# Negated maximum as bias of four exps, and value products of attention in groups, in a post-norm decoder layer

## The chip, the cores and the metric

The kernel runs on one core of a Trainium2 chip. The metric is the device time of one launch in microseconds. Before the change it is 2332.79 us, the median of three runs (2332.78 to 2335.61).

The engines of a core are called here as the profile calls them: PE (matrix products, with its weight loads as PEld), DVE (vector engine), ACT (scalar engine), POOL (GpSimd), SP (the queue that issues DMAs). Each works through its own list of instructions in order; semaphores tie the lists together.

## The reference

One decoder layer on 32 batch items of 256 tokens with 256 features; all activations are float32.

```python
x = _layernorm(x + self_attention(x))            # 16 heads of 16, causal, with biases
x = _layernorm(x + cross_attention(x, ctx))      # 16 heads of 64, 77 context tokens
x = _layernorm(x + ffn(x))                       # weights of +1/-1: 512->1024->1024->256, relu twice

# cross attention, per head
scores = jnp.einsum('bhqd,bhkd->bhqk', q, k) * scale      # scale = 64 ** -0.5
attn = jax.nn.softmax(scores, axis=-1)                    # over 77 keys
out = jnp.einsum('bhqk,bhkd->bhqd', attn, v)
```

## The kernel before, in words

A first part (about 140 us) loads and splits the weights and computes keys and values of the context for all 32 items. Then `attention(i, f, g)` runs once per item `i`, 32 times. One pass of it holds, interleaved by hand, the self attention and the cross attention of item `i`, the scores of the self attention of item `i + 1`, two layers of the feed-forward part of item `f = i - 1` and the last layer of item `g = i - 2`. Each engine has its own function `attention`, and the order of the calls in it is that engine's order of work. Nothing else sets the order: there is no scheduler. The feed-forward products (`layer0`, `layer1`, `layer2`, called through `filler0`, `filler2` and `layer1_until`) stand where PE would otherwise wait.

The cross attention of an item works on eight blocks `t` of two heads with 256 queries, so that one block has 4 rows of 77 scores in each of 128 partitions. For a block these functions follow each other, one engine handing to the next:

- PE `cross_queries(u)` (L988, two blocks at a time), ACT `cross_queries(u)` copies them out of PSUM (L499).
- PE `cross_scores(t)` (L1130) writes PSUM bank 4 or 5 in turn, so block `t` can start when block `t - 2` has left its bank.
- DVE `cross_max(t)` (L736) and `cross_below(t)` (L742): the maximum, and scores minus maximum into `p2`. The second frees the bank (semaphore `d_b2`).
- ACT `cross_exp(t)` (L504) on `p2` in place, DVE `cross_sum(t)` (L748) and `cross_inverse(t)` (L753), POOL the product with the inverse (L419).
- PE `cross_transposes(t)` (L1141), ACT `cross_probs(t)` copies them out (L511), PE `cross_values(t)` (L1155), ACT `cross_output(u)` (L516) and DVE `cross_output_low(u)` (L758) for two blocks, PE `cross_projection(t)` (L1169).

`cross_values` has 77 rows by 64 columns of weights: head 0 of a block lands in the left half of PE's columns, head 1 in the right half. `values(g)` of the self attention (L1082) has 32 columns of weights, four heads side by side. The other products use all 128 columns, the transposes of L1141 77 of them.

In the self attention, PE `scores_by_key(n)` (L1069), ACT `self_probs(n)` (L524) and POOL (L412) make the probabilities of two heads in one of four buffers `pr`, and `values(g)` uses two of them.

Of the kernel before, what the change touches and what calls it, by code (L numbers as in the profile page):

```python
# [14 lines left out]
P = 128  # L15
# [10 lines left out]
def decoder_layer(nc, x, ctx, w_qkv, b_qkv, w_proj, b_proj, w_q, w_k, w_v, w_o, k0, k1, k2, s0, s1, s2, out):  # L26
# [22 lines left out]
    with ExitStack() as stack:  # L49
# [31 lines left out]
        max2 = sb("max2", [P, KX, 4], F32)  # L81
# [14 lines left out]
        with ExitStack() as first:  # L96
# [20 lines left out]
        probs = sb("probs", [P, 6, 512], F32)  # L117
        probs_flat = probs[:].rearrange("p a b -> p (a b)")
        pr = probs_flat[:, 0:4 * 768].rearrange("p (n a b) -> p n a b", n=4, a=2)
# [10 lines left out]
        p2 = sb("p2", [P, KX, 4, SK], F32)  # L130
        p2_t = sb("p2_t", [SK, 4, 512], F32)
# [49 lines left out]
        d_m2, d_b2, d_s2, d_i2, d_o2l, d_y2, d_x2, d_r0, d_r1, d_y3, d_out = (  # L181
            sem("d_" + n) for n in "m2 b2 s2 i2 o2l y2 x2 r0 r1 y3 out".split())
# [49 lines left out]
        SPLIT_SCALE = (1.0, 1.0, 1.0, CROSS_SCALE, 1.0)  # L232
# [149 lines left out]
        def _(pool):  # L382
# [24 lines left out]
            def attention(i, f, g, more=True):  # L407
                for n in range(NP):
                    pool.wait_ge(a_p, nth(i, NP, n + 1))
                    pool.sem_inc(passed_pool, 1)  # L410
                    diag = pr[:, n % 4, :, 0:2 * P].rearrange("p a (b q) -> p a b q", b=2)
                    pool.affine_select(out=diag, in_=diag, compare_op=ALU.is_ge, fill=0.0, base=0,  # L412
                                       pattern=[[0, 2], [0, 2], [1, P]], channel_multiplier=-1).then_inc(g_p, 1)
# [29 lines left out]
        def _(act):  # L443
# [74 lines left out]
            def self_probs(i, n):  # L518

                act.wait_ge(pe_st, nth(i, NP, n + 1))  # L520
                if n >= 4:
                    act.wait_ge(pe_pv, nth(i, 4, n // 2 - 1))
                b = 4 + 2 * (n % 2)
                act.activation(pr[:, n % 4, :, :], ps[:, b:b + 2, P:512], ACT.Exp, scale=SELF_SCALE).then_inc(a_p, 1)  # L524

            def self_output(i, m):

                act.wait_ge(pe_pv, nth(i, 4, 2 * m + 2))
# [7 lines left out]
            def attention(i, first, f, first_f=False, more=True):  # L536
# [98 lines left out]
        def _(dve):  # L635
# [126 lines left out]
            def attention(i, first, f, g, more=True):  # L762
# [9 lines left out]
                self_output(i, 0)  # L772
                if more:
                    transposed_x(i + 1)
                if not first:
# [28 lines left out]

                cross_max(i, 0)
                cross_below(i, 0)
                cross_max(i, 1)
                cross_below(i, 1)
                cross_sum(i, 0)
                if more:  # L810
                    self_max(i + 1, 0)
                for t in range(2, KX):
                    cross_max(i, t)
                    cross_inverse(i, t - 2)
                    cross_below(i, t)
# [118 lines left out]
        def _(pe):  # L934
# [138 lines left out]
            def values(i, g):  # L1073

                pe.wait_ge(g_p, nth(i, NP, 2 * g + 2))
                if g == 0:
                    pe.wait_ge(a_nm, nth(i, 2, 2))
                c = (g % 2) * S
                for b in range(TB):
                    for j in range(4):  # L1080
                        src = pr[:, (2 * g + j // 2) % 4, j % 2, (1 - b) * P:(3 - 2 * b) * P]
                        last = pe.matmul(ps[32 * j:32 * j + 32, 2 + g // 2, c + b * P:c + S], v[:, b, 4 * g + j, :], src,  # L1082
                                         start=b == 0, stop=b == 1)
# [39 lines left out]
            def cross_scores(i, t):  # L1123
# [3 lines left out]
                if t >= 2:  # L1127
                    pe.wait_ge(d_b2, nth(i, KX, t - 1))
# [16 lines left out]
            def cross_values(i, t):  # L1145

                u = t // 2
                pe.wait_ge(a_p2t, nth(i, KX, t + 1))
                if t % 2 == 0 and u < 2:
                    pe.wait_ge(a_q2, nth(i, 4, u + 3))  # L1150
                elif t % 2 == 0:
                    pe.wait_ge(a_o2h, nth(i, 4, u - 1))
                    pe.wait_ge(d_o2l, nth(i, 4, u - 1))
                for e in range(2):
                    last = pe.matmul(ps[64 * e:64 * e + 64, 6 + u % 2, (t % 2) * S:(t % 2 + 1) * S],  # L1155
                                     v2[:, (2 * t + e) * XD:(2 * t + e + 1) * XD], p2_t[:, t % 4, e * S:(e + 1) * S],
                                     start=True, stop=True)
                last.then_inc(pe_o2, 1)

            def cross_projection(i, t):  # L1160

                if t == 0:
                    pe.wait_ge(d_b2, nth(i, KX, KX))
# [19 lines left out]
            def attention(i, f, g, more=True):  # L1183
# [18 lines left out]
                values(i, 0)  # L1202
                filler2(2)
                scores_by_key(i, 4)
                if f is not None:
                    if g is not None:
                        pe.wait_ge(d_y3, nth(g, 2, 1))
                    transposed_x2(f)
# [176 lines left out]
```

## Time and profile before

| | |
|---|---|
| median of three runs | 2332.79 us |
| the profiled execution | 2333.06 us |
| its span, first to last instruction | 2331.3 us |
| mean granted clock of PE in it | 0.987 |
| PE busy | 2233.6 us, 96% of the span |
| DVE busy | 1485.0 us, 64% |
| ACT busy | 970.2 us, 42% |
| POOL busy | 482.0 us, 21% |

"Busy" counts the time in which at least one instruction of the engine is under way. PE's matmuls overlap in the records, since the next one starts while the results of the last still run out of the array; what an instruction costs PE is therefore read from the distance between two starts, not from its duration. On ACT and DVE also the next instruction starts before the last has ended, by about 0.1 us.

In the rows below `ps` is PSUM, `p` is the cross attention's `p2`, `p_t` its transpose, `q` the tile `q2`; `x8` means eight instructions merged into one row. A bracket at a row's end is idle time before it, and who ended it.

### The profile page before, as it was taken

How to read it: one execution, taken by the hardware profiler on the slowest of the kernel's cores; microseconds unless marked ns; L12 is line 12 of the kernel's file. 1: busy time of each engine (PE TensorE's matmuls, PEld its weight loads, DVE VectorE, ACT ScalarE, POOL GpSimd, SP SyncE). 2: the span in 40 equal slices, each digit the busy share in tenths (PEclk: the TensorE clock that was granted, in tenths of full speed). 3: DMA queues.
4: the chain of work that ended last, by engine and by line, in shares of the span. 5: the costliest groups of instructions: out<-in, count | busy, mean ns of one | idle time of the engine just before them, and what ended most of it. 6: DMA issues, size and time to landing. Idle time of an engine off the chain costs nothing.

```text
span 2331.3 us, 52778 instructions
## 1 busy us (share of the span) xinstructions
PE 2233.6 (96%) x18516; PEld 1847.7 (79%) x18516; DVE 1485.0 (64%) x4685; ACT 970.2 (42%) x1797; POOL 482.0 (21%) x751
## 2 busy tenths in 40 slices
PE   7967899999999999999999999999999999999997
PEld 6856787888888888788888888888888888888876
DVE  3435666667667666667676666676676666676763
ACT  3313444444444444444444444444444444444432
POOL 2001212222222122212222222222221222122220
PEclk9978999999999999999999999999999999999999
DMA  6753332132333331233333322323333212233300
GB/s 209 228 115 53 54 58 45 39 50 37 56 56 56 56 50 41 42 44 49 56 56 56 56 42 39 47 41 56 56 56 56 48 40 44 40 53 56 56 25 10
DMA packets 150504, 135.85 MB, mean 58 GB/s; under 512 B 47746, under 2 KB 141986, under 8 KB 150402
## 3 DMA queue, kind: packets, MB, share of 16 engines
q1 hardware_dynamic: 150468, 135.37, 31.3%
q8 instruction: 23, 0.38, 0.1%
q14 instruction: 13, 0.11, 0.0%
HBM read 39.10 MB, written 28.59 MB: 29 GB/s over the span
## 4 chain that ended last, share of the span: by engine, by line
PE 81%; DVE 10%; issue 4%; ACT 3%; DMA 2%; POOL 1%; SPq 0%; DVEq 0%; POOLq 0%
PE ps L1028 10%; PE ps L1029 9%; PE ps L1169 9%; PE ps L988 8%; PE ps L1155 6%; PE ps L1011 5%; PE ps L1141 4%; PE ps L1082 4%; PE ps L1069 4%; PE ps L997 4%; DVE max L736 3%; PE ps L1039 3%; PE ps L1040 2%; PE ps L970 2%; PE ps L977 2%
## 5 line engine op out<-in xcount | busy, mean ns | idle before, releaser
L1028 PE MATMUL ps<-r_h,w 128*128 128x256 f16 x2048 | 464.4, 274 | 1.9 <-DVE r_l L682 1.9
L1029 PE MATMUL ps<-r_l,w 128*128 128x256 f16 x2048 | 462.1, 273 | 0.0
L471 ACT ACTIVATE r_h<-ps 128x512 f16<-128x512 f32 x256 | 152.6, 596 | 524.1 <-PE ps L1029 516.4
L697 DVE CUSTOM_DVE_ANT_0 junk<-ps,causal 128x128 bf16<-128x128 f32 (+1 forms) x1024 | 316.2, 353 | 60.1 <-PE ps L1058 53.8
L419 POOL TENSOR_TENSOR p<-p,inv 128x308 f32<-128x308 f32 x256 | 179.0, 699 | 479.5 <-DVE inv L753 479.5
L682 DVE SCALAR_TENSOR_TENSOR r_l<-ps,r_h 128x512 f16<-128x512 f32 x256 | 176.1, 688 | 119.5 <-ACT r_h L471 119.5
L524 ACT ACTIVATE probs<-ps 128x768 f32<-128x768 f32 x256 | 206.9, 809 | 106.9 <-PE ps L1069 106.8
L412 POOL TENSOR_SCALAR_AFFINE_SELECT probs<-probs 128x512 f32<-128x512 f32 x256 | 163.3, 638 | 393.8 <-ACT probs L524 393.7
L1028 PEld LDWEIGHTS ps<-r_h,w 128*128 128x128 f16 x2048 | 200.1, 98 | 49.6 <-issue 23.5
L1029 PEld LDWEIGHTS ps<-r_l,w 128*128 128x128 f16 x2048 | 200.9, 98 | 20.7
L758 DVE TENSOR_TENSOR o_l<-ps,o_h 128x512 fp32r<-128x512 f32 x128 | 88.5, 691 | 191.0 <-ACT o_h L516 190.6
L429 POOL TENSOR_SCALAR var_eps<-mv 128x2 f32<-128x2 f32 x96 | 20.9, 217 | 831.9 <-DVE mv L671 831.9
L1069 PE MATMUL ps<-q_st,k_bd 128*128 128x256 f32 x1024 | 186.3, 306 | 3.1 <-DMA q_st<-neg_max 3.1
L504 ACT ACTIVATE p<-p 128x308 f32<-128x308 f32 x256 | 117.5, 459 | 166.3 <-DVE p L742 166.3
L1130 PE MATMUL ps<-k_bd,q 128*128 128x154 f32 x1024 | 176.6, 305 | 10.0 <-DVE p L742 5.5
L511 ACT ACTIVATE p_t<-ps 77x512 f32<-77x512 f32 x256 | 149.1, 583 | 72.3 <-PE ps L1141 72.3
L1130 PEld LDWEIGHTS ps<-k_bd,q 128*128 128x128 f32 x1024 | 143.6, 189 | 42.1 <-issue 33.9
L1155 PE MATMUL ps<-p_t,v 77*64 77x256 f32 x1024 | 167.0, 405 | 0.0
L1141 PE MATMUL ps<-ident,p 128*77 128x128 f32 x1024 | 158.4, 277 | 6.7 <-ACT p_t L511 6.7
L736 DVE TENSOR_REDUCE max<-ps 128x4 f32<-128x308 f32 x256 | 120.7, 471 | 52.7 <-PE ps L1130 52.7
L1141 PEld LDWEIGHTS ps<-ident,p 128*77 128x77 f32 x1024 | 120.3, 147 | 40.5 <-issue 25.9
L1069 PEld LDWEIGHTS ps<-q_st,k_bd 128*128 128x128 f32 x1024 | 141.0, 194 | 7.8 <-issue 4.1
(140 smaller groups left out, 4729.3 us busy)
## 6 DMA issues: line engine op xcount, KB each, us to landing
q_st<-o_h SPq DMA_DIRECT2D x192, 128.0 KB
k_bd<-o_h SPq DMA_DIRECT2D x192, 128.0 KB, 6.7
q<-q SPq DMA_DIRECT2D x128, 128.0 KB, 2.1
v_scratch<-v_out SPq DMA_DIRECT2D x44, 224.0 KB, 2.3
k_bd<-k_scratch SPq DMA_DIRECT2D x64, 154.0 KB
v<-v_scratch SPq DMA_DIRECT2D x32, 308.0 KB
x_in<-in_x SPq DMA_DIRECT2D x32, 256.0 KB, 4.6
out<-y SPq DMA_DIRECT2D x32, 256.0 KB, 2.2
```

The costliest lines, as they stand in the source:

```text
L419: pool.tensor_tensor(p2[:, t], p2[:, t], inv2[:, t, :].unsqueeze(2).to_broadcast([P, 4, SK]), ALU.mult).then_inc(g_p2, 1)
L524: act.activation(pr[:, n % 4, :, :], ps[:, b:b + 2, P:512], ACT.Exp, scale=SELF_SCALE).then_inc(a_p, 1)
L697: dve.tensor_tensor_reduce(out=junk[:, e, b * P:b * P + width], in0=ps[:, bank + b, e * width:(e + 1) * width], in1=causal[:, (1 - b) * P: ...
L736: dve.tensor_reduce(max2[:, t, :], ps[:, 4 + t % 2, 0:4 * SK].rearrange("p (j k) -> p j k", j=4), AX_X, ALU.max).then_inc(d_m2, 1)
L988: last = pe.matmul(dst, w[:, kk, cols], a[:, kk, :], start=kk == 0 and n == 0, stop=kk == KD - 1 and n == 2)
L1028: pe.matmul(dst, w1[:, kk, m * P:(m + 1) * P], r0_h[:, kk, :], start=kk == 0, stop=False)
L1029: last = pe.matmul(dst, w1[:, kk, m * P:(m + 1) * P], r0_l[:, kk, :], start=False, stop=kk == KF - 1)
L1069: last = pe.matmul(ps[:, 4 + 2 * (n % 2) + e, (1 - kb) * S:(2 - kb) * S], k_bd[:, n, e, kb * P:(kb + 1) * P], q_st[:, n, :], start=True, s ...
L1130: last = pe.matmul(ps[:, 4 + t % 2, b * 2 * SK:(b + 1) * 2 * SK], q2[:, t, b * P:(b + 1) * P], k2_bd[:, t, :], start=True, stop=True)
L1141: last = pe.transpose(ps[0:SK, 2 + t % 2, e * S + b * P:e * S + (b + 1) * P], p2[:, t, 2 * b + e, :], ident[:])
L1155: last = pe.matmul(ps[64 * e:64 * e + 64, 6 + u % 2, (t % 2) * S:(t % 2 + 1) * S], v2[:, (2 * t + e) * XD:(2 * t + e + 1) * XD], p2_t[:, t ...
L1169: last = pe.matmul(ps[:, 4 + b, 0:D], a[:, t, b * P:(b + 1) * P], w[:, t, :], start=t == 0 and n == 0, stop=t == KX - 1 and n == 2)
```

## The change

It has four parts.

1. DVE no longer subtracts. `cross_low(t)` (in place of `cross_max`) takes the minimum over scores whose sign is turned (the query weights are scaled by `-CROSS_SCALE`), which is the negated maximum. ACT `cross_exp(t)` then reads the scores from PSUM in four instructions of 77 elements, one per row of scores, with `scale=-1.0` and this minimum as bias. The bank is freed by the last of the four (semaphore `a_e2`), and `cross_scores` waits for that.
2. `cross_values(u)` does two blocks at once, so that it is called four times and not eight. It waits for the copies of both blocks.
3. `values(m)` does four pairs of heads at once, two calls and not four. For this there are six probability buffers and not four, two of them in `p2`.
4. Some calls change place in the lists: ACT `cross_output(0)` stands ahead of `cross_probs(3)`; `cross_output(1)` and `(2)` move up likewise, `self_probs(7)` stands ahead of a relu; DVE `transposed_x(i + 1)` ahead of `self_output(i, 0)`, and `self_max(i + 1, 0)` ahead of `cross_sum(i, 0)`.

```diff
-        SPLIT_SCALE = (1.0, 1.0, 1.0, CROSS_SCALE, 1.0)
+        SPLIT_SCALE = (1.0, 1.0, 1.0, -CROSS_SCALE, 1.0)
...
             def cross_exp(i, t):
-                act.wait_ge(d_b2, nth(i, KX, t + 1))
-                act.activation(p2[:, t], p2[:, t], ACT.Exp).then_inc(a_e2, 1)
+                act.wait_ge(d_m2, nth(i, KX, t + 1))
+                for j in range(4):
+                    last = act.activation(p2[:, t, j, :], ps[:, 4 + t % 2, j * SK:(j + 1) * SK], ACT.Exp,
+                                          bias=low2[:, t, j:j + 1], scale=-1.0)
+                last.then_inc(a_e2, 1)
...
-            def cross_below(i, t):
-                dve.wait_ge(d_m2, nth(i, KX, t + 1))
-                dve.tensor_tensor(p2[:, t], ps[:, 4 + t % 2, 0:4 * SK].rearrange("p (j k) -> p j k", j=4),
-                                  max2[:, t, :].unsqueeze(2).to_broadcast([P, 4, SK]), ALU.subtract).then_inc(d_b2, 1)
...
                 for t in range(2, KX):
-                    cross_max(i, t)
+                    cross_low(i, t)
                     cross_inverse(i, t - 2)
-                    cross_below(i, t)
                     cross_sum(i, t - 1)
...
             def cross_scores(i, t):
                 if t >= 2:
-                    pe.wait_ge(d_b2, nth(i, KX, t - 1))
+                    pe.wait_ge(a_e2, nth(i, KX, t - 1))
```

On ACT, in the cross stage of an item, these are the instructions before (`L499` query copies, `L504` exps, `L511` copies of transposes, `L516` outputs):

```order
L499 ACTIVATE q<-ps 128x512 x2
L504 ACTIVATE p<-p 128x308
L499 ACTIVATE q<-ps 128x512
L504 ACTIVATE p<-p 128x308 x2
L499 ACTIVATE q<-ps 128x512
L504 ACTIVATE p<-p 128x308 x2
L511 ACTIVATE p_t<-ps 77x512
L504 ACTIVATE p<-p 128x308
L511 ACTIVATE p_t<-ps 77x512
```

and the same stretch now, with other line numbers (`L503` queries, `L509` exps, `L518` copies):

```order
L503 ACTIVATE q<-ps 128x512 x2
L509 ACTIVATE p<-ps,low 128x77 x4
L503 ACTIVATE q<-ps 128x512
L509 ACTIVATE p<-ps,low 128x77 x8
L503 ACTIVATE q<-ps 128x512
L509 ACTIVATE p<-ps,low 128x77 x8
L518 ACTIVATE p_t<-ps 77x512
L509 ACTIVATE p<-ps,low 128x77 x4
L518 ACTIVATE p_t<-ps 77x512
```

The sequence of blocks is the same; each exp has become four. On PE, from the transposes of block 2 to those of block 4, with the semaphores that each waits for, before:

```order
L1141 MATMUL ps<-ident,p 77x128 [waits a_p2t,g_p2]
L1141 MATMUL ps<-ident,p 77x128 x3
L1155 MATMUL ps<-p_t,v 64x256 [waits a_q2,a_p2t]
L1155 MATMUL ps<-p_t,v 64x256
L1130 MATMUL ps<-k_bd,q 128x154 [waits d_b2]
L1130 MATMUL ps<-k_bd,q 128x154
L1057 MATMUL ps<-k_bd,q_st 128x256 [waits d_mx]
L1058 MATMUL ps<-k_bd,q_st 128x512
L1141 MATMUL ps<-ident,p 77x128 [waits a_p2t,g_p2]
L1141 MATMUL ps<-ident,p 77x128 x3
L1155 MATMUL ps<-p_t,v 64x256 [waits a_p2t]
L1155 MATMUL ps<-p_t,v 64x256
```

and now (`L1140` transposes, `L1154` values, `L1129` cross scores, `L1055` and `L1056` self scores):

```order
L1140 MATMUL ps<-ident,p 77x128 [waits a_p2t,g_p2]
L1140 MATMUL ps<-ident,p 77x128 x3
L1154 MATMUL ps<-p_t,v 64x256 [waits a_q2,a_p2t]
L1154 MATMUL ps<-p_t,v 64x256 x3
L1129 MATMUL ps<-k_bd,q 128x154 [waits a_e2]
L1129 MATMUL ps<-k_bd,q 128x154
L1140 MATMUL ps<-ident,p 77x128 [waits a_p2t,g_p2]
L1140 MATMUL ps<-ident,p 77x128 x3
L1055 MATMUL ps<-k_bd,q_st 128x256 [waits d_mx]
L1056 MATMUL ps<-k_bd,q_st 128x512
```

Here the values of block 1 have moved up to those of block 0, and the scores of block 7 stand behind both; they wait for ACT's exps (`a_e2`) where they waited for DVE's subtraction (`d_b2`).

## Rows read from the trace of the kernel before

**Rows 1.** The page, part 1: busy us, share of the span, instructions.

```profile
PE 2233.6 (96%) x18516; PEld 1847.7 (79%) x18516; DVE 1485.0 (64%) x4685; ACT 970.2 (42%) x1797; POOL 482.0 (21%) x751
```

**Rows 2.** Waits: who waited for whom, total us, times, longest.

```profile
PE ps L1130 <- DVE p L742: 5.5, 29, 0.2
```

**Rows 3.** Timeline of PE, a cross stage: start us, us, engine, line, operation.

```profile
1205.88 1.21 PE L1130 MATMUL ps<-k_bd,q 128*128 128x154 f32 x8
1206.82 0.50 PE L988 MATMUL ps<-xt_h,wq_h 128*128 128x256 f32 x2
...
1209.62 0.50 PE L988 MATMUL ps<-xt_h,wq_h 128*128 128x256 f32 x2
...
1211.48 0.76 PE L1130 MATMUL ps<-k_bd,q 128*128 128x154 f32 x4 [0.19 <-DVE p L742]
...
1212.67 0.79 PE L1130 MATMUL ps<-k_bd,q 128*128 128x154 f32 x4
...
1219.42 0.66 PE L1141 MATMUL ps<-ident,p 128*77 128x128 f32 x4
1220.01 0.65 PE L1155 MATMUL ps<-p_t,v 77*64 77x256 f32 x4
```

**Rows 4.** The same timeline, later: values between projections.

```profile
1225.02 0.40 PE L1169 MATMUL ps<-wo_h,o_l 128*128 128x256 f32 x2
...
1226.27 0.40 PE L1169 MATMUL ps<-wo_l,o_h 128*128 128x256 f32 x2
1226.51 0.40 PE L1169 MATMUL ps<-wo_h,o_l 128*128 128x256 f32 x2
...
1227.41 0.51 PE L1169 MATMUL ps<-wo_h,o_h 128*128 128x256 f32 x2
```

**Rows 5.** Timeline of PE in the self attention.

```profile
1252.87 0.38 PE L1011 MATMUL ps<-x2t_l,w 128*128 128x256 f16 x2
1253.18 0.86 PE L1082 MATMUL ps<-probs,v 128*32 128x256 f32 x16
1253.97 0.39 PE L1011 MATMUL ps<-x2t_h,w 128*128 128x256 f16 x2
```

**Rows 6.** Groups by line and form: busy us, mean ns of one, idle before.

```profile
L524 ACT ACTIVATE probs<-ps 128x768 f32<-128x768 f32 x256 | 206.9, 809 | 106.9 <-PE ps L1069 106.8
...
L736 DVE TENSOR_REDUCE max<-ps 128x4 f32<-128x308 f32 x256 | 120.7, 471 | 52.7 <-PE ps L1130 52.7
...
L481 ACT ACTIVATE o_h<-ps,bias_qk 128x256 fp32r<-128x256 f32 x128 | 53.7, 470 | 55.5 <-PE ps L988 55.5
```

**Rows 7.** Timeline of ACT.

```profile
1208.53 0.60 ACT L499 ACTIVATE q<-ps 128x512 f32<-128x512 f32 x1 [0.44 <-PE ps L988]
1209.02 0.45 ACT L504 ACTIVATE p<-p 128x308 f32<-128x308 f32 x1
1211.37 0.46 ACT L504 ACTIVATE p<-p 128x308 f32<-128x308 f32 x1 [1.89 <-DVE p L742]
1211.73 0.58 ACT L499 ACTIVATE q<-ps 128x512 f32<-128x512 f32 x1
...
1218.37 0.57 ACT L511 ACTIVATE p_t<-ps 77x512 f32<-77x512 f32 x1
1218.85 0.58 ACT L516 ACTIVATE o_h<-ps 128x512 fp32r<-128x512 f32 x1
...
1258.97 0.84 ACT L481 ACTIVATE o_h<-ps,bias_qk 128x256 fp32r<-128x256 f32 x2 [0.81 <-PE ps L988]
```

**Rows 8.** Timeline of DVE in the cross stage.

```profile
1210.85 0.48 DVE L742 TENSOR_TENSOR p<-ps,max 128x308 f32<-128x308 f32 x1
...
1212.13 0.48 DVE L742 TENSOR_TENSOR p<-ps,max 128x308 f32<-128x308 f32 x1
```

**Rows 9.** Windows: stretch, length, busy us by engine, granted clock, DMA, GB/s.

```profile
245.00:250.00 5.00, 3.50 (x15) 2.77 (x15) 3.68 (x24) 1.18 (x2) 1.54 (x2) 0.53 0.01 2
2301.00:2306.00 5.00, 2.69 (x24) 1.93 (x22) 2.68 (x6) 2.23 (x5) 0.85 (x2) 1.00 0.15 52
```

More of the change, by code:

```diff
@@ L180, in decoder_layer @@
             sem("d_" + n) for n in "xt qk v x2t mx rc on ol y1 x1 x1t".split())
-        d_m2, d_b2, d_s2, d_i2, d_o2l, d_y2, d_x2, d_r0, d_r1, d_y3, d_out = (
-            sem("d_" + n) for n in "m2 b2 s2 i2 o2l y2 x2 r0 r1 y3 out".split())
+        d_m2, d_s2, d_i2, d_o2l, d_y2, d_x2, d_r0, d_r1, d_y3, d_out = (
+            sem("d_" + n) for n in "m2 s2 i2 o2l y2 x2 r0 r1 y3 out".split())
         d_bn = [sem(f"d_bn{n}") for n in range(3)]
@@ L1071, in scores_by_key, with values @@
                 last.then_inc(pe_st, 1)
-            def values(i, g):
-                pe.wait_ge(g_p, nth(i, NP, 2 * g + 2))
-                if g == 0:
+            def values(i, m):
+                pe.wait_ge(g_p, nth(i, NP, 4 * m + 4))
+                if m == 0:
                     pe.wait_ge(a_nm, nth(i, 2, 2))
[L1078 to L1083, printed above, removed]
+                for g in (2 * m, 2 * m + 1):
+                    c = (g % 2) * S
+                    for b in range(TB):
+                        for j in range(4):
+                            src = pr(2 * g + j // 2)[:, j % 2, (1 - b) * P:(3 - 2 * b) * P]
+                            last = pe.matmul(ps[32 * j:32 * j + 32, 2 + m, c + b * P:c + S], v[:, b, 4 * g + j, :], src,
+                                             start=b == 0, stop=b == 1)
                 last.then_inc(pe_pv, 1)
@@ L1143, in cross_transposes, with cross_values @@
                 last.then_inc(pe_p2t, 1)
[L1145 to L1149, printed above, removed]
+            def cross_values(i, u):
+                pe.wait_ge(a_p2t, nth(i, KX, 2 * u + 2))
+                if u < 2:
                     pe.wait_ge(a_q2, nth(i, 4, u + 3))
-                elif t % 2 == 0:
+                else:
                     pe.wait_ge(a_o2h, nth(i, 4, u - 1))
                     pe.wait_ge(d_o2l, nth(i, 4, u - 1))
[L1154 to L1158, printed above, removed]
+                for t in (2 * u, 2 * u + 1):
+                    for e in range(2):
+                        last = pe.matmul(ps[64 * e:64 * e + 64, 6 + u % 2, (t % 2) * S:(t % 2 + 1) * S],
+                                         v2[:, (2 * t + e) * XD:(2 * t + e + 1) * XD], p2_t[:, t % 4, e * S:(e + 1) * S],
+                                         start=True, stop=True)
+                    last.then_inc(pe_o2, 1)
             def cross_projection(i, t):
                 if t == 0:
-                    pe.wait_ge(d_b2, nth(i, KX, KX))
+                    pe.wait_ge(a_e2, nth(i, KX, KX))
                 if t % 2 == 0:
@@ L1208, in attention @@
                     transposed_x2(f)
+                values(i, 0)
                 scores_by_key(i, 5)
                 filler2(3)
[L1211 removed]
+                scores_by_key(i, 6)
                 filler0(0)
[L1213 removed]
+                scores_by_key(i, 7)
                 filler0(1)
[L1215 to L1216 removed]
                 if more:
@@ L1223, in attention @@
                 filler0(3)
-                values(i, 3)
+                values(i, 1)
                 filler0(4)
```

60 lines of the change are left out of this document (25 added, 35 removed).

## The prediction

> **What bounds the kernel now.** I read the busy shares first, then who waited for whom, then the timelines of the engines through one cross stage. PE is busy 96% of the span [rows 1], and the waits view gives it no large wait: the most regular one that this change touches is that of the cross scores for DVE's subtraction, 29 times, 5.5 us in all [rows 2]. So the kernel is bound by PE's list, item after item. Two things change the time: what PE's list costs when nobody keeps it waiting, and waits that are added to it. What DVE, ACT or POOL spend matters only where PE waits for it. Because one cross stage is like the next (256 blocks, eight to an item, hence 32 items [rows 6]), I work out one item from its timeline and multiply by 32. Times of the walk below are those of the timeline with 1200 taken off: 9.02 is 1209.02.
>
> **Grouping the values: a gain on PE.** Between two projections that follow each other without anything between, their pairs of products start 0.24 apart (1226.27 and 1226.51). From the pair at 1225.02 to the second pair after the value block, at 1226.27, it is 1.25; with two such pairs taken off, the value block costs 0.78 [rows 4]. How much of this is streaming? The granted clock in the loop is at the upper of its two levels, 2.4 GHz (1.00). Two score blocks of four 154-column instructions cost 0.94 (5.88 to 6.82 [rows 3]) and about 0.1 more at the first product behind them (a pair there lasts 0.50 and not 0.40): 1.04 / 8 / 154 is 0.84 ns a column, two passes at that clock. Four instructions of 256 columns would then take 0.86 one after the other, and 0.43 where two stand side by side in the two halves of the columns. Since the whole block costs 0.78, they do run side by side, and 0.35 is the price of going into this form and out of it again. A merged block pays it once. For the self values: from the pair at 1252.87 to that at 1253.97 it is 1.10; less one pair of f16 products (0.22) it is 0.88; the streaming of four heads side by side, 256 and then 128 columns, four passes in all, is 0.64. So the overhead is 0.24 [rows 5]. The change takes away two self blocks of four: 2 x 0.24 = 0.48 us an item. It takes away four cross blocks of eight, but the first two merges lie ahead of a wait that decides (below), so their gain is swallowed; the last two give 2 x 0.35 = 0.70.
>
> The Trainium skill, TensorEngine Tiling, section Key Properties, says that changing the tiling mode drains the engine. The trace agrees with its 0.35 and 0.24 us; by that rule this part of the change is a pure gain.
>
> **The exps: a cost on ACT, in PE's way.** The trace has no 77-element exp with a bias from memory. The nearest row is L481: PSUM source, a bias per partition, 256 elements, 470 ns [rows 6], two of them in 0.84 [rows 7], so the second starts 0.37 after the first. An element costs 0.83 ns (0.81 us for 768, 0.60 for 512 [rows 6, 7]). Without a bias, 308 elements from SBUF occupy ACT for 0.36 (11.37 to 11.73), 512 from PSUM for 0.48 (18.37 to 18.85) [rows 7]: 0.26 + 0.10 and 0.43 + 0.05. L481 has 0.21 for its elements, so 0.16 fixed in its spacing and 0.26 in its duration. With 77 elements (0.064) that is 0.22 spacing and 0.32 duration. Four of them: done after 3 x 0.22 + 0.32 = 0.98, ACT free after 0.88; before it was 0.46 and 0.36. Bounds: without any price of the bias the spacing is 0.064 + 0.05 = 0.115 and the last one takes 0.23, so done after 0.58, free after 0.46; with no overlap at all 4 x 0.32 = 1.28 for both. I take 0.98 and 0.88, since L481 has the same source and the same kind of bias.
>
> The Trainium skill, ScalarE: Activation LUTs, section What ACT_TABLE_LOAD costs, prices each pointer operand at about 93 ns, 280 ns + 0.833 ns an element in all, with 93 ns of overlap. The trace has this with a somewhat smaller constant, 0.26 for 0.28. By the page's figures (an estimate) four exps are done after 1.09 and the kernel would come to 2378 us.
>
> The latency of a block is not worse for that: maximum, subtraction and exp were 0.47 + 0.48 + 0.46, minimum and four exps are 0.47 + 0.98. What is worse is where they stand. The bank of the scores was free after DVE's subtraction; now it waits for ACT, whose list puts query copies, copies of transposes and outputs between the exps. Walk, with 0.03 for a hand-over to DVE or ACT (an estimate), 0.10 for one to PE (the subtractions ending at 11.33 and 12.61 [rows 8] let PE start at 11.48 and 12.67 [rows 3], 0.15 and 0.06):
> - Exp 1 stands behind query copy 2 and starts at 9.02 as before [rows 7]. Done 10.00; scores 3 start at 10.10 (9.15 before, the second half of a pair of score blocks that ends at 9.62). PE goes on to queries 3 at 10.57 and not 9.62.
> - Query copy 3 follows 1.71 after the start of its queries (6.82 to 8.53 [rows 3, 7]): 12.28. Exp 3 stands behind it, 0.49 later: 12.77, done 13.75. Scores 5 start at 13.85 (12.67 before).
> - They take 0.79 and 0.03, the minimum 0.47 and 0.03: exp 5 at 15.17, copy 1 behind it at 16.05, done (0.58) 16.63. The merged values 0 and 1 now need it: 16.73. They cost 0.58 + 0.43 = 1.01, so scores 7 start at 17.74.
> - 0.82 and 0.50 on: exp 7 at 19.06, output 0 at 19.94, copy 3 at 20.42 (0.48 spacing), done 21.01, and the merged values 2 and 3 wait for it: 21.11.
> - Behind that PE has no late partner: copies 4 to 7 and outputs 1 to 3 come in time by 0.2 us or more. Before, values 3 started at 20.01 and projection 4 at 27.41, 7.40 later [rows 3, 4]. Now that stretch also holds the transposes 5 (0.59) and one more streaming (0.43) and saves two merges (0.70): 7.72. Projection 4 starts at 28.83: **1.42 us later**.
>
> In this walk PE waits some 3.3 us in the stage, where it had waited about 1.
>
> DVE loses eight subtractions of 0.48 an item. Worth nothing: behind the two first blocks DVE's partner is ACT, and PE does not wait for its sums (the transposes are ready each time before PE gets there). Moving the self maximum ahead of the sum, the six buffers, the moved relu and `transposed_x` I put at nothing: the self stage has all its waits met by 0 to 0.4 us; if that cover goes, 0.1 to 0.2 us an item. DMAs stay as they are.
>
> **Sum.** 1.42 - 0.48 = +0.94 us an item, x 32 = 30 us. On the profiled execution's 2333.06 us (0.3 over the median) that is 2363 us.
>
> **Rivals.**
> - *The exps run closer together than L481 says* (ends on the other side). With 0.115 and 0.23 the two "done" terms of the walk shrink by 0.40 each and the two "free" terms by 0.42: 1.64 less, 1.42 becomes -0.22, with the self stage -0.70 an item, -22 us: **2311 us**. The point of balance is a spacing of 0.153 us. For: 0.05 is the fixed part of every exp from PSUM without bias [rows 7]. Against: L481 has 0.16, with a bias. The same sign comes if the orders of ACT's list hurt less than I walk, for the walk ends 0.94 above zero and has four hand-overs in it.
> - *No overlap between the four, or merges that save nothing.* 1.28 for both puts 1.40 on the walk: +2.34 an item, **2408 us**. Merges worthless: 0.70 + 0.48 + 0.16 more: +2.28, **2406 us**. Against: L481 overlaps; the 0.35 shows directly.
> - *The clock.* A stage with waits could pull PE to 1.2 GHz: at 245 to 250 us the granted clock is 0.53, with PE busy 3.50 of 5.00 us. But at 2301 to 2306 us it is busy 2.69 of 5.00 and keeps 1.00 [rows 9], and the stage here would be busy three quarters with no wait over 1.5 us. One dip of 3 us an item would double that stretch and give some 2450 us. 3 in 100.
> - *No change*: the effects balance within 5 us.
>
> **Chances and range.** Forecast, 2345 to 2385 us: 58 in 100. Faster rival: 25. Balance: 5. Beyond 2385 (the second and third rival together): 12. The range goes from 2308 to 2385: some 8 below, 12 above. Within 0.2% (about what a measurement of this kernel can tell from no change) 5 in 100, faster 25, slower 70.
>
> **What would show it.** The exps of 77 elements: mean near 320 ns, spacing near 0.22, ACT's busy time up by some 130 us (256 x 0.52). DVE's down by 122. In PE's waits new large rows: value products (L1154) and scores (L1129) for ACT, 2 to 3 us an item. Distance of two value blocks merged: 1.01. A busy PE, no such waits and a shorter period would prove the first rival. The distance from item to item should grow by 0.9 us. I am wrong if the spacing of the exps is under 0.15, or if PE gets copy 3 before it has finished transposes 4.

## The result, and the profile after

The changed kernel takes 2354.4 us (median of four runs, 2350.4 to 2355.8) against 2334.2 us (2332.8 to 2336.9) for the kernel before on the same chip: ratio 1.0078, 95% interval 1.0065 to 1.0091. It is 20 us slower, where 30 were forecast. Its profiled span is 2351.3 us against 2331.3, at a mean granted clock of 0.986 (0.987 before).

The page of the changed kernel, part 1 (busy us, share, instructions):

```profile
PE 2179.6 (93%) x18516; PEld 1864.2 (79%) x18516; DVE 1397.7 (59%) x4429; ACT 1095.0 (47%) x2565; POOL 480.8 (20%) x751
```

PE is busy 54 us less than before and the kernel is slower: the share has fallen from 96% to 93% [rows 1]. That is the sign of new waits. The waits view of the changed kernel names them (total us, times, longest):

```profile
PE ps L1154 <- ACT p_t L518: 62.2, 64, 1.7
PE ps L1129 <- ACT p L509: 29.9, 64, 1.0
```

Two waits of the value products for ACT's copies of the transposes and two of the scores for ACT's exps, in each of 32 items: 92.1 us, 2.9 an item. The small wait for DVE's subtraction [rows 2] has gone. PE's timeline through the cross stage shows where they sit (start us, us, engine, line; in the bracket the idle time before the row and who ended it). Take 1207.80 off to compare with the walk: the stage starts at 5.88 in both.

```profile
1213.68 1.21 PE L1129 MATMUL ps<-k_bd,q 128*128 128x154 f32 x8
...
1217.84 0.79 PE L1129 MATMUL ps<-k_bd,q 128*128 128x154 f32 x4 [0.68 <-ACT p L509]
1218.37 0.50 PE L986 MATMUL ps<-xt_h,wq_h 128*128 128x256 f32 x2
...
1221.58 0.79 PE L1129 MATMUL ps<-k_bd,q 128*128 128x154 f32 x4 [0.23 <-ACT p L509]
...
1224.41 1.08 PE L1154 MATMUL ps<-p_t,v 77*64 77x256 f32 x8 [0.64 <-ACT p_t L518]
1225.43 0.79 PE L1129 MATMUL ps<-k_bd,q 128*128 128x154 f32 x4
...
1228.75 1.08 PE L1154 MATMUL ps<-p_t,v 77*64 77x256 f32 x8 [1.31 <-ACT p_t L518]
1229.76 0.66 PE L1140 MATMUL ps<-ident,p 128*77 128x128 f32 x4
1230.18 0.48 PE L1168 MATMUL ps<-wo_h,o_h 128*128 128x256 f32 x2
...
1234.94 0.40 PE L1168 MATMUL ps<-wo_h,o_l 128*128 128x256 f32 x2
...
1236.28 0.50 PE L1168 MATMUL ps<-wo_h,o_h 128*128 128x256 f32 x2
1236.62 0.40 PE L1168 MATMUL ps<-wo_l,o_h 128*128 128x256 f32 x2
```

The rows of before that answer to these are [rows 3, 4]. Read in the way of [rows 4], between two projections, a merged value block of eight instructions costs 1.21 (1234.94 to 1236.62 is 1.68, less two pairs of 0.235), where two single ones cost 2 x 0.78 = 1.56. ACT's timeline over the same stretch (same columns) gives the reason for each bracket:

```profile
1216.33 0.60 ACT L503 ACTIVATE q<-ps 128x512 f32<-128x512 f32 x1 [0.44 <-PE ps L986]
1216.83 0.96 ACT L509 ACTIVATE p<-ps,low 128x77 f32<-128x77 f32 x4
...
1220.07 0.60 ACT L503 ACTIVATE q<-ps 128x512 f32<-128x512 f32 x1
1220.56 1.87 ACT L509 ACTIVATE p<-ps,low 128x77 f32<-128x77 f32 x8
...
1222.92 0.97 ACT L509 ACTIVATE p<-ps,low 128x77 f32<-128x77 f32 x4
1223.76 0.60 ACT L518 ACTIVATE p_t<-ps 77x512 f32<-77x512 f32 x1
...
1226.77 0.97 ACT L509 ACTIVATE p<-ps,low 128x77 f32<-128x77 f32 x4 [1.08 <-DVE low L743]
1227.61 0.61 ACT L523 ACTIVATE o_h<-ps 128x512 fp32r<-128x512 f32 x1
1228.09 1.09 ACT L518 ACTIVATE p_t<-ps 77x512 f32<-77x512 f32 x2
```

The first: exp 1 starts at 1216.83 behind query copy 2 and ends at 1217.79; scores 3 start 0.05 later. The last: ACT idles for 1.08 us ahead of exp 7. Its list lets nothing else through, and when exp 7 starts at 1226.77 the transposes of block 3 have been done for 0.1 us (they start at 1226.06 and take 0.60). Yet copy 3 stands behind exp 7 and output 0 in the list and starts at 1228.09. PE waits 1.31 us for that copy.

The chain of waits has the group of 24 query products at the head of each item (start us, us, what). After:

```profile
1211.04 2.81 PE ps L986 x24
```

Its follower in the next item starts 66.61 us later, at 1277.65. In the kernel before the same two stand at 1203.23 and 1269.37, 66.14 apart. So an item costs 0.47 us more here, and 0.49 in the mean over 29 items. The 20.0 us of span are made of: 1.4 us by which the third item starts later, 29 x 0.49 = 14.3, and 4.3 in the last item. There the next item's self scores, which fill PE elsewhere, are missing; the waits are up to 1.65 us, and the granted clock falls:

```profile
2292.96 1.08 PE L1154 MATMUL ps<-p_t,v 77*64 77x256 f32 x8 [1.65 <-ACT p_t L518]
...
2302.02 0.51 PE L1168 MATMUL ps<-wo_h,o_h 128*128 128x256 f32 x2
```

The distances part the two. From the start of the cross stage to projection 4 the last item takes 19.92 us in the kernel before (2262.18 to 2282.10) and 24.12 in the changed one (2277.90 to 2302.02): 4.20 apart, where the loop has 21.53 and 22.60, 1.07 apart. The kernel before gets 1.61 shorter in its last item, since the fill, and DVE's self maximum that goes with it, are gone. The changed kernel gets nothing for it: up to values 2 it takes 15.06 and in the loop 15.07, for ACT's chain sets this time and not PE's work. And from values 2 to projection 4 the same instructions take 9.06 (the two rows above) for 7.53 in the loop (1228.75 to 1236.28): 1.53 us for the clock, which is granted at 0.50 from 2294 to 2297 us. 1.07 + 1.61 + 1.53 is the 4.2.

Windows of the changed kernel, one in the loop and three at its end (stretch, length, busy us of PE, PEld, DVE, ACT, POOL, granted clock, DMA share, GB/s):

```profile
1223.00:1228.00 5.00, 3.80 (x29) 2.73 (x27) 2.68 (x9) 3.92 (x15) 2.50 (x4) 1.00 0.00 0
...
2285.00:2290.00 5.00, 3.77 (x28) 2.80 (x27) 2.79 (x9) 4.83 (x19) 2.10 (x3) 1.00 0.00 0
2290.00:2295.00 5.00, 3.35 (x25) 2.59 (x24) 2.63 (x8) 3.00 (x8) 2.06 (x3) 0.89 0.01 3
2295.00:2300.00 5.00, 5.00 (x34) 4.16 (x34) 1.10 (x2) 2.09 (x4) 0.00 (x0) 0.77 0.00 0
```

### The profile page after: what moved, and what is told of

Same layout as the page of the kernel before. It is cut to its first block, busy times and chain, and to the rows that moved or that the text cites. A ratio compares the mean times of both kernels' runs of the same rounds, so it can differ in the third digit from the quotient of the medians.

```text
span 2351.3 us, 53255 instructions
## 1 busy us (share of the span) xinstructions
PE 2179.6 (93%) x18516; PEld 1864.2 (79%) x18516; DVE 1397.7 (59%) x4429; ACT 1095.0 (47%) x2565; POOL 480.8 (20%) x751
## 4 chain that ended last, share of the span: by engine, by line
PE 82%; ACT 11%; DVE 3%; issue 1%; DMA 1%; POOL 1%; SPq 0%; DVEq 0%; POOLq 0%; ACTq 0%
PE ps L986 12%; PE ps L1026 9%; PE ps L1027 9%; PE ps L1168 8%; ACT p L509 6%; PE ps L1154 6%; PE ps L1009 5%; PE ps L1067 4%; PE ps L1081 4%; PE ps L995 4%; PE ps L1129 4%; PE ps L1037 3%; PE ps L968 2%; PE ps L1038 2%; PE ps L955 2%; PE ps L975 2%
## 5 line engine op out<-in xcount | busy, mean ns | idle before, releaser
L509 ACT ACTIVATE p<-ps,low 128x77 f32<-128x77 f32 x1024 | 245.7, 330 | 87.7 <-DVE low L743 87.0
L1129 PE MATMUL ps<-k_bd,q 128*128 128x154 f32 x1024 | 183.2, 306 | 33.4 <-ACT p L509 29.9
L743 DVE TENSOR_REDUCE low<-ps 128x4 f32<-128x308 f32 x256 | 121.8, 476 | 138.2 <-PE ps L1129 135.1
L1129 PEld LDWEIGHTS ps<-k_bd,q 128*128 128x128 f32 x1024 | 144.7, 189 | 67.2 <-ACT p L509 57.0
L1154 PE MATMUL ps<-p_t,v 77*64 77x256 f32 x1024 | 138.8, 392 | 62.2 <-ACT p_t L518 62.2
L416 POOL TENSOR_SCALAR_AFFINE_SELECT probs<-probs 128x512 f32<-128x512 f32 x192 | 122.5, 638 | 282.3 <-ACT probs L531 282.2
L531 ACT ACTIVATE probs<-ps 128x768 f32<-128x768 f32 x192 | 154.6, 806 | 52.6 <-PE ps L1067 47.2
L518 ACT ACTIVATE p_t<-ps 77x512 f32<-77x512 f32 x256 | 150.0, 602 | 42.6 <-PE ps L1140 42.6
L1140 PE MATMUL ps<-ident,p 128*77 128x128 f32 x1024 | 156.3, 276 | 0.0
L1154 PEld LDWEIGHTS ps<-p_t,v 77*64 77x64 f32 x1024 | 62.1, 136 | 105.1 <-ACT p_t L518 77.0
```

Source lines behind the costliest of these rows:

```text
L509: last = act.activation(p2[:, t, j, :], ps[:, 4 + t % 2, j * SK:(j + 1) * SK], ACT.Exp, bias=low2[:, t, j:j + 1], scale=-1.0)
L1129: last = pe.matmul(ps[:, 4 + t % 2, b * 2 * SK:(b + 1) * 2 * SK], q2[:, t, b * P:(b + 1) * P], k2_bd[:, t, :], start=True, stop=True)
L1140: last = pe.transpose(ps[0:SK, 2 + t % 2, e * S + b * P:e * S + (b + 1) * P], p2[:, t, 2 * b + e, :], ident[:])
```

## The experiments

Each ratio is to the kernel before on the same chip. "Item" is the distance between two of those query groups at about 1200 us: 66.14 before, 66.61 after.

**First round: the change taken apart.**

*e1_exps_only.* The kernel before with the four exps alone; values and lists as they were.

```diff
- act.wait_ge(d_b2, ...)
- act.activation(p2[:, t], p2[:, t], ACT.Exp)
+ act.wait_ge(d_m2, ...)
+ for j in range(4):
+     act.activation(p2[:, t, j, :], ps[:, 4 + t % 2, j * SK:(j + 1) * SK], ACT.Exp, bias=low2[:, t, j:j + 1], scale=-1.0)
```

> The kernel before with only the four biased exps (minimum on DVE, bank freed by ACT); values ungrouped, all orders as before. Theory A (the loss comes from the two together: a late copy of transposes costs PE little while each value block waits for one copy alone, and much once a merged block waits for two): a walk gives projection 0 at 0.36 us behind before, so about +0.4 us an item, 2346 us. Theory B (the four exps alone carry the loss, and grouping is a gain of 1.3 to 1.9 us an item wherever it stands): without the groups the time is above that of the changed kernel, 2395 to 2414 us.

Measured: 2348.4 us, ratio 1.0052 (1.0034 to 1.0069), item 66.47, +0.33.

```profile
PE ps L1124 <- ACT p L505: 41.0, 64, 1.0
```

The exps alone make the kernel slower, by the wait of the scores for the exp that now frees their bank: 64 times, two an item.

*e2_groups_only.* The changed kernel with DVE's subtraction and the single exp put back (the reverse of the edit above); values grouped, ACT's list as changed.

> The changed kernel with the subtraction on DVE and the single exp put back; all value groups and the new orders stay. Theory A: the merged values 0 and 1 still wait for copy 1 (walk: 16.24 on the clock of the item), scores 7 come 1.1 us late behind them, copy 3 comes late, values 2 and 3 start near 20.6; projection 4 is 0.7 us late and the self stage gains 0.5 to 0.6: +0.1 us an item, 2333 to 2342 us. Theory B: every merge gains, 1.3 to 1.9 us an item, 2274 to 2292 us.

Measured: 2341.8 us, ratio 1.0023 (1.0014 to 1.0033), item 66.22, +0.08.

```profile
PE ps L1160 <- ACT p_t L515: 60.3, 64, 1.7
```

The groups alone bring nothing either: they make eight instructions wait for the later of two copies, 64 times. (DVE's list has sum 0 ahead of the self maximum again, as in the kernel before; so it has in e8.) The two halves, 0.33 and 0.08, add up to 0.41 of the whole 0.47.

*e3_self_groups.* As e2, but with the cross values and both lists of the cross stage as in the kernel before; only the self values are grouped. The moves that the change makes in the self stage (`self_probs(7)`, `transposed_x`) are in it too.

> As the run with groups only, but the cross values ungrouped and PE's and ACT's cross lists as before: only the self values are grouped. Theory A: nothing in the self stage is made to wait, so two column-mode blocks fewer give 2 x 0.24 to 0.29 us an item: 2315 to 2319 us. Theory B gives the same. A rival that puts the price of a block down to its own instructions and not to the change of form expects 2334 us, no change.

Measured: 2317.2 us, ratio 0.9924 (0.9902 to 0.9946), item 65.57, -0.57. The waits view shows no wait in the loop that was not there before. The groups and the two moves are not measured apart.

*e4_late_merges.* e3, and the last two pairs of cross values side by side in PE's list, with nothing else moved.

```diff
  cross_values(i, 4)
+ cross_values(i, 5)
  ...
- cross_values(i, 5)
  ...
- cross_values(i, 6)
  ...
+ cross_values(i, 6)
  cross_values(i, 7)
```

> As the run with self groups only, and on PE the values 4 with 5, and 6 with 7 stand side by side (values 0 to 3 single, single exp). Theory A: these two merges have no late partner and give 2 x 0.35 us an item more: 2291 to 2298 us, faster than both kernels. The rival that gives the change of form no price expects no gain over the self groups.

Measured: 2296.0 us, ratio 0.9825 (0.9809 to 0.9841), item 64.86, which is 0.71 less than e3. Two merges save two times 0.35, the price read from [rows 4]. e2 holds everything of e4, the first two merges and the moved outputs on ACT, and costs 1.36 us an item more. Output 0 ahead of copy 3 has its share in this: in the changed kernel it holds ACT for 0.48 (1227.61 to 1228.09) just when PE waits for that copy. No run parts it from the merges; together they lose more than two merges in time save.

**Second round: the exp's size, and its place.** All four on one chip.

*e5_one_exp.* The changed kernel with one exp of 308 elements and one bias instead of four; this leaves out the minimum of rows 1 to 3 in each block.

```diff
- for j in range(4):
-     last = act.activation(p2[:, t, j, :], ..., bias=low2[:, t, j:j + 1], scale=-1.0)
+ act.activation(p2[:, t], ps[:, 4 + t % 2, 0:4 * SK]..., ACT.Exp, bias=low2[:, t, 0:1], scale=-1.0)
```

> The changed kernel with one exp of 308 elements a block, still from PSUM with a bias, in place of four of 77 (all four rows of scores get the first row's minimum, so the softmax of the other three is shifted by a wrong constant). Theory A (ACT's time for a block of exps, 0.97 to the last result and 0.88 until ACT is free, puts the waits on PE): 0.51 and 0.42; walk: scores 3 at 9.63, scores 5 at 12.9, merged values 0 and 1 at 15.3, merged values 2 and 3 at 19.2 for 20.95: 1.7 to 1.8 us an item less than the changed kernel, 2294 to 2302 us. Theory C (the cost is that exps read PSUM and hold the bank until ACT has read it, not their number): at most 0.3 us an item less, 2345 us or more.

Measured: 2296.3 us, ratio 0.983 (0.9813 to 0.9846), item 64.83. Even with the short exp PE waits 34.3 us for the copies of the transposes: that is the order of ACT's list and the merges, without the price of the exps.

*e6_no_bias.* Four exps, but without their bias operand; this leaves out the minimum.

```diff
- bias=low2[:, t, j:j + 1], scale=-1.0)
+ scale=-1.0)
```

> The changed kernel, four exps a block as before but without the bias operand (the minimum is still computed and waited for, and not subtracted). If the fixed part of 0.15 in the spacing is the bias operand's, the spacing falls from 0.215 to about 0.115 and the last one takes 0.23: done after 0.58, free after 0.46, about 1.6 us an item less by the walk, some 2300 us. If it is the price of any short instruction, the spacing stays near 0.2 and the time near 2350 us.

Measured: 2306.3 us, ratio 0.9875 (0.9859 to 0.9892), item 65.20. The same group in both kernels (busy us, mean ns, idle before), then four exps on ACT's timeline without the bias:

```profile
L509 ACT ACTIVATE p<-ps,low 128x77 f32<-128x77 f32 x1024 | 245.7, 330 | 87.7 <-DVE low L743 87.0
```

```profile
L509 ACT ACTIVATE p<-ps 128x77 f32<-128x77 f32 x1024 | 157.1, 242 | 119.5 <-DVE low L743 118.4
```

```profile
1258.13 0.61 ACT L509 ACTIVATE p<-ps 128x77 f32<-128x77 f32 x4 [0.44 <-DVE low L743]
```

With bias the spacing is (0.97 - 0.33) / 3 = 0.21 us, without it (0.61 - 0.24) / 3 = 0.12: 0.09 us an exp is the bias operand's, and the means, 330 and 242 ns, say the same. The item falls by 1.41 us, and the waits with it:

```profile
PE ps L1154 <- ACT p_t L518: 39.6, 64, 1.3
...
PE ps L1129 <- ACT p L509: 11.0, 33, 0.7
```

This is the first rival of the prediction made real: it put a spacing of 0.115 us at 2311 us and -0.70 an item, and 0.12 measures 2306 and -0.94. The rival's sum was sound in sign and near in size, only its premise did not hold.

*e7_exps_reordered.* The changed kernel with nothing but ACT's list in another order (e exp, q query copy, c copy of transposes, o output; the first two query copies stay ahead):

```diff
- e0 q2 e1 e2 q3 e3 e4 c0 e5 c1 e6 c2 e7 o0 c3 c4 o1 c5 c6 o2 c7 o3
+ e0 e1 q2 e2 e3 q3 e4 c0 c1 e5 c2 e6 o0 c3 e7 c4 o1 c5 c6 o2 c7 o3
```

> The changed kernel with ACT's list alone in another order in the cross stage: exp 1 ahead of query copy 2, exp 3 ahead of query copy 3, copies 0 and 1 ahead of exp 5, output 0 and copy 3 ahead of exp 7. ACT's work and PE's list stay. Theory A (the loss is where the exps stand in ACT's list): scores 3 at 9.15, scores 5 at 13.2, values 0 and 1 at 15.75, values 2 and 3 at 18.85 for 20.95: 2.1 us an item less, 2283 to 2292 us, and the last item loses its dip of the clock. Theory D (ACT simply has too much to do in the stage): the same waits in other places, 2345 to 2355 us.

Measured: 2304.0 us, ratio 0.9862 (0.9846 to 0.9879), item 65.11. The waits for the copies are gone and 1.5 us an item with them, but 2283 to 2292 were expected. PE's timeline shows what took their place:

```profile
1199.46 0.76 PE L1129 MATMUL ps<-k_bd,q 128*128 128x154 f32 x4 [1.06 <-ACT p L509]
...
1207.99 0.48 PE L1168 MATMUL ps<-wo_h,o_h 128*128 128x256 f32 x2 [0.33 <-DVE o_l L759]
```

Scores 4 now wait 1.06 us for exp 2, which is done late because its minimum stands behind the self maximum in DVE's list; and the first projection waits for DVE, whose list has sum 7 ahead of the low part of output 0. I had moved ACT's list and left DVE's as it was. (Both waits go when DVE's list is moved, in e10b and e11.) The last item is as expected: the granted clock stays at 1.00 in it, and from the start of its cross stage to the kernel's end it takes 69.0 us, where the changed kernel takes 73.4 and the kernel before 69.1.

*e8_groups_reordered.* e2 (subtraction on DVE, one exp) with copies 0, 1 and 2 ahead of exps 4, 5 and 6, and output 0 and copy 3 ahead of exp 7 on ACT. Unlike in e7, exps 1 and 3 stay behind query copies 2 and 3.

> The kernel with groups and the single exp after DVE's subtraction (2342 us), with ACT's list alone in another order: copy 0 ahead of exp 4, copy 1 ahead of exp 5, copy 2 ahead of exp 6, output 0 and copy 3 ahead of exp 7. Theory A: values 0 and 1 at 15.2, values 2 and 3 at 18.5 for 20.6, projection 0 0.5 us earlier than in the first kernel: 1.9 us an item less, 2275 to 2285 us, faster than every kernel so far. If merged cross values cost PE waits wherever they stand, it stays above the 2296 us of the kernel with the two late merges.

Measured: 2267.7 us, ratio 0.9707 (0.969 to 0.9723), item 64.00. Against e2 the order of ACT's list alone is worth 2.2 us an item: the waits view has no wait of the values for ACT in the loop any more. It came out better than expected, and it beats e4 by 0.86 us an item. That fits two more merges at 0.35 each which nothing swallows, with 0.16 left for ACT's order; no run has this order without the two merges.

**Third round: DVE's list as well.** Is DVE's relief, which I had put at nothing, worth something when ACT is in order?

*e9b_single_exp_dve.* e8 with DVE's list reordered: maxima and subtractions of blocks 2 and 3, sum 1 and inverses 0 and 1 ahead of the self maximum.

> The fastest kernel so far (groups, DVE's subtraction, single exp, ACT's list reordered; 2267.7 us), with DVE's list reordered too: maxima and subtractions of blocks 2 and 3 and the sums of 0 and 1 ahead of the self maximum. Theory A: the wait of scores 4 (0.35 us from the end of queries 3) goes, 0.3 to 0.4 us an item less, 2254 to 2259 us. If PE's remaining waits in this stage have another cause, 2265 to 2268 us.

Measured: 2274.8 us, ratio 0.9742 (0.9725 to 0.9758): slower than e8, a miss. DVE's and PE's timelines:

```profile
1249.82 0.47 DVE L740 TENSOR_REDUCE max<-ps 128x4 f32<-128x308 f32 x1
1250.21 0.17 DVE L757 RECIPROCAL inv<-sum 128x4 f32<-128x4 f32 x1
1250.33 0.48 DVE L746 TENSOR_TENSOR p<-ps,max 128x308 f32<-128x308 f32 x1
```

```profile
1250.95 0.76 PE L1154 MATMUL ps<-k_bd,q 128*128 128x154 f32 x4 [1.03 <-DVE p L746]
```

From 1246.98 to 1250.81 DVE has no gap over 0.03 us: cross maxima, sums and subtractions and the self maximum stand end to end, and PE's scores 6 wait 1.03 us for the last subtraction. With the subtraction on it, DVE is full over this stretch, and what was moved ahead of the self maximum made subtraction 4 late. This is one other order of DVE's list; that none would help is not shown.

*e10b_four_exps_dve.* e7 with DVE's list reordered in a like way (minima 2 and 3, sums 0 and 1 and inverses 0 and 1 ahead of the self maximum), output 0's low part ahead of sum 7, and c0 ahead of e4.

> The changed kernel with its four biased exps and ACT's list reordered (2304.0 us), with DVE's list reordered too: minima of blocks 2 and 3 ahead of the self maximum, output low 0 ahead of sum 7; copy 0 ahead of exp 4 on ACT. Theory A: the wait of scores 4 (1.1 us) and that of projection 0 (0.3 us) go: projection 0 at 19.8 for 20.9, 1.1 us an item less, 2265 to 2272 us, so that the four exps, well placed, come within 0.7% of the single exp. If ACT is simply full, the waits move on and it stays above 2290 us.

Measured: 2256.0 us, ratio 0.9666 (0.9644 to 0.9687), item 63.63: better than expected. What is left is one wait an item for an exp:

```profile
PE ps L1143 <- ACT p L509: 21.3, 32, 0.7
```

**Fourth round: the two designs side by side.** Five runs of each, on one chip.

*e11_four_exps_final.* e10b with that wait taken away: minimum 4 right behind the self maximum on DVE, exp 4 ahead of copy 0 on ACT, so that ACT's list is that of e7. DVE's list against the changed kernel (l minimum, s sum, i inverse, S self maximum, o output low):

```diff
- l0 l1 S s0 l2 i0 s1 l3 i1 s2 l4 i2 s3 l5 i3 s4 l6 i4 s5 l7 i5 s6 i6 s7 o0 i7
+ l0 l1 s0 i0 l2 s1 l3 i1 S l4 s2 i2 l5 s3 i3 s4 i4 l6 s5 i5 l7 s6 i6 o0 s7 i7
```

> The kernel with four biased exps and reordered lists (2256.0 us), with minimum 4 put directly behind the self maximum on DVE and exp 4 ahead of copy 0 on ACT. Its one wait left in the stage, scores 6 for exp 4 (0.66 us an item), should shrink to 0.2 at most: 0.4 to 0.5 us an item less, 2240 to 2246 us. If DVE or ACT only shift the wait to the transposes 2 or the values 0 and 1, 2252 us or more.

Measured: 2245.0 us (2244.3 to 2247.5), ratio 0.962 (0.9606 to 0.9633), item 63.24. It beats the kernel before by 89 us on the same chip, and the changed kernel's 2354.4 by 109. The time is as expected; the wait fell from 0.66 to 0.28 us and not to 0.2, and the item by 0.39.

```profile
PE 2156.6 (96%) x18516; PEld 1859.2 (83%) x18516; DVE 1409.5 (63%) x4429; ACT 1081.3 (48%) x2565; POOL 480.8 (21%) x751
```

*e12_single_exp_again.* The kernel of e8 beside it.

> The kernel with groups, DVE's subtraction, the single exp and ACT's list reordered, measured once more beside the kernel with four exps on the same chip: 2264 to 2271 us as before, so that the ratio of the two tells whether the four exps are worth having once the lists fit them (20 to 30 us, about 1%).

Measured: 2268.3 us (2268.2 to 2269.6), ratio 0.9719 (0.9705 to 0.9732). So the best version with four exps is 23 us ahead of the best that I found with the subtraction. The two differ in exps, in ACT's list and in DVE's, and the side with four exps had one more round of reordering, so the 23 us are those of these two kernels. Where does the difference lie? PE's timeline of e8, from the second pair of score blocks on:

```profile
1179.00 1.21 PE L1135 MATMUL ps<-k_bd,q 128*128 128x154 f32 x8
...
1181.81 0.76 PE L1135 MATMUL ps<-k_bd,q 128*128 128x154 f32 x4 [0.19 <-DVE p L746]
1182.40 0.60 PE L1146 MATMUL ps<-ident,p 128*77 128x128 f32 x4
1182.99 0.79 PE L1135 MATMUL ps<-k_bd,q 128*128 128x154 f32 x4
1183.62 0.60 PE L1146 MATMUL ps<-ident,p 128*77 128x128 f32 x4
1184.36 0.76 PE L1135 MATMUL ps<-k_bd,q 128*128 128x154 f32 x4
```

and of e11:

```profile
1229.94 1.21 PE L1143 MATMUL ps<-k_bd,q 128*128 128x154 f32 x8
...
1232.39 0.68 PE L1143 MATMUL ps<-k_bd,q 128*128 128x154 f32 x4
1232.92 0.60 PE L1154 MATMUL ps<-ident,p 128*77 128x128 f32 x4
1233.35 0.69 PE L1143 MATMUL ps<-k_bd,q 128*128 128x154 f32 x4
1233.88 0.60 PE L1154 MATMUL ps<-ident,p 128*77 128x128 f32 x4
1234.76 0.76 PE L1143 MATMUL ps<-k_bd,q 128*128 128x154 f32 x4 [0.28 <-ACT p L509]
```

Read the distances between the starts. From the pair of score blocks to the first single block e8 takes 2.81 us and e11 2.45; from there to the second 1.18 and 0.96; to the third 1.37 and 1.41. Together e8 is 0.54 us behind, of the 0.76 us between the two items. In e8 transposes are followed after 0.59 and 0.74 us where 0.43 is possible (1232.92 to 1233.35 in e11): PE stands still ahead of scores whose bank DVE's subtraction frees. DVE's timeline bears it out: the subtractions of blocks 2, 3 and 4 end at 1181.66, 1182.94 and 1184.22, and scores 4, 5 and 6 start 0.15, 0.05 and 0.14 later. The waits view lists only the 0.19, since the last results still run out of the array in the other gaps.

## Why the prediction was right, and where its size was off

**What bounds the kernel: right.** PE's list, item after item, plus the waits that are added to it. e4 takes time off PE's list alone, and e3 nearly so, and the time follows.

**The price of the column form: right for the cross values, low for the self values.** 0.35 us a block was taken from one value block between projections [rows 4]; e4 gives 0.71 for two, and the merged block of the changed kernel 1.21 for 1.56. For the self values 2 x 0.24 = 0.48 was taken [rows 5]; e3 gives 0.57, and the changed kernel's self stage is 0.58 shorter. The Trainium skill, TensorEngine Tiling (Array Packing), section Key Properties, says that a change of the tiling mode drains the engine. e3 and e4 agree with it in so far as such a change has a price, 0.28 and 0.35 us a block; that the price is a drain no run here shows.

**Which merges pay: right, and this decided.** The first two were to be swallowed by ACT's copies 1 and 3, and e2 shows them in two waits an item. e8, where these copies come earlier and all four merges stay, has neither wait and is 2.2 us an item faster: it was the lateness of the copies, and nothing in the merge.

**The exps: right.** Spacing 0.22 taken, 0.21 measured; mean 320 ns taken, 330 measured. ACT's busy time grew by 124.8 us where 130 were said. Of the choice between the bounds, e6 shows the reason: the bias operand costs 0.09 us. The lower bound's fixed part of 0.05 was said to be that of exps, but it was read from a copy (1218.37 to 1218.85); e6 gives 0.06 for exps. And the point of balance comes out of the prediction's own figures as 0.16 us (0.22 less 0.94 / 1.64 of the 0.105 between the bounds), not 0.153; nothing hangs on it. The Trainium skill, ScalarE: Activation LUTs, section What ACT_TABLE_LOAD costs, gives about 93 ns for a pointer operand, and e6 agrees. Its sum for one instruction, 280 ns + 0.833 ns an element, makes 344 ns of 77 elements, where 330 were measured. The 2378 us that the prediction worked out for the kernel from these figures were 24 too high, of which 9 are in the prediction's own 2363 as well.

**The walk: right in its places, 0.35 us too long in its sum.** It named four waits: scores 3 and 5, values 0 and 1, values 2 and 3. All four are there, and the waits view has no other in the stage. (By the distances, scores 4 too start 0.27 late, 0.51 behind a pair that takes 0.24; before it was 0.35, and it costs nothing here, since scores 5 wait for exp 3 anyway.) Walk and trace (1207.80 taken off): scores 3 at 10.10 and 10.04, exp 3 at 12.77 and 12.76, scores 5 at 13.85 and 13.78, exp 5 at 15.17 and 15.12, values 0 at 16.73 and 16.61, scores 7 at 17.74 and 17.63, exp 7 at 19.06 and 18.97, values 2 at 21.11 and 20.95, projection 4 at 28.83 and 28.48. Two terms were mis-sized. The hand-overs to PE were taken at 0.10 and are nearer 0.05; with small shares of exps and copies they make the 0.16 at values 2. And the transposes of block 5 behind the merged values were put at 0.59, the distance in the kernel before [rows 3], and take 0.42 (1229.76 to 1230.18): the old 0.59 held the way into the column form, which the merge has already removed. Elsewhere in the changed kernel transposes between two projections take 0.35 (1233.32 to 1233.67), and ahead of a value block 0.53 (1230.97 to 1231.50), 0.18 more. I counted the merge's gain and kept a cost that belonged to it. That is 0.17 to 0.19 us.

**The sum.** +1.42 - 0.48 = +0.94 us an item was forecast; +1.07 - 0.58 = +0.49 came. 32 items would give 15.7 us. The rest of the 20 is 0.4 in the first two items (1.4 for 2 x 0.49) and 3.8 in the last (4.3 for 0.49), where I had taken all items as alike; the clock rival, at 3 in 100 for the loop, came true once there, in one item and not in 32, and cost 1.5 us. So the item was forecast at nearly twice what it costs, and the total comes nearer (20 for 30) only because some 4 us came from places that were put at nothing: that part of the agreement is luck. The sign, the places of the waits and both halves of the sum are not: without those 4 us the time would be about 2350, on the same side.

**DVE's relief: right for this kernel, wrong as a general word.** "Worth nothing" holds as long as ACT is late. Once ACT's list is in order, the subtraction is what PE waits for (e8, e9b), and e11, without it and with DVE's list in order as well, gains 23 us on e12. Without that order the relief did not show even then: in e7, with DVE's list as it was, scores 4 wait 1.06 us an item. DVE's busy time fell by 87 us and not by 122: a subtraction overlaps the end of the instruction ahead of it, and the next one overlaps its own end. In the kernel before the inverse ahead of subtraction 2 ends at 1210.91 and the sum behind it starts at 1211.25; only these 0.34 us are the subtraction's alone, and 256 x 0.34 is 87 us.

**Rivals.** Exps closer together: refuted in its premise (0.21 and not 0.115), borne out in sign and nearly in size by e6. No overlap: refuted, four exps take 0.97 and not 1.28. Merges worthless: refuted by e4. No change: refuted, the ratio's interval from 1.0065 to 1.0091 leaves 1 out.

What stays open: why the first two items gather 0.4 us more than two of the loop (from 250 to 255 us the granted clock is 0.50 in the changed kernel and 0.79 before, from 255 to 260 us 0.88 and 1.00; no run parts this from the rest), and what part of the 3.8% below is the reordering alone. The groups account for 0.57 + 4 x 0.35 = 1.97 of the 2.90 us an item between the first kernel and e11. The other 0.93 belong to four exps and reordered lists together, and no run reorders the first kernel's lists by themselves, though PE waits in its stage too, by about 1 us an item as the prediction reads it.

## What to carry to other kernels

When work moves from one engine to another, ask first what stands ahead of it in the receiver's in-order list and who waits behind it; its busy share (ACT had 42%) says nothing about that. Group products in a tiled form only where the last operand of the group is there in time: the first two merges, with an output moved ahead of the copy that they need, cost 1.36 us an item in one order of ACT's list, and the kernel that has them was 0.86 ahead in another. And judge such a move only after the lists of all engines on the chain have been put in order again: as written this change costs 0.8%, and with ACT's and DVE's lists reordered the kernel is 3.8% faster than the first.

## What the runs showed of the hardware that I had not expected

- More than half of the fixed price of a short exp in a row of them is its bias operand: of the 0.21 us spacing 0.06 are the elements' and 0.09 the bias operand's (e6).
- At the end of the changed kernel PE was busy 3.77 of 5.00 us at a granted clock of 1.00, then 3.35 at 0.89, then 5.00 at 0.77: means of stretches at 2.4 and at 1.2 GHz (from 2294 to 2297 us it is 0.50). The waits before the fall were 1.02, 0.59, 0.64 and 1.65 us. In the loop a stretch that is busy 3.80 of 5.00 us, with waits of 0.64 and, right behind it, 1.31 us, keeps 1.00 all along (the first row of the windows above), and so does the last item of e2, with 0.55 and 1.67 us.
- A gap of 0.3 us between matmuls can be missing from the waits view; distances between starts showed it (e8).
